# A post-norm layer kernel: the order of its last three chunks rearranged on VectorE, ScalarE and GpSimd

## What is computed

```python
# mixer: a gated linear recurrence over time, then RMS norm and a projection
r = sigmoid(x @ Wr.T); k = x @ Wk.T; v = x @ Wv.T
scale = exp(t * log(sigmoid(decay)))
state = cumsum(k * v / clip(scale, 1e-10)) * scale
x = layernorm(x + rmsnorm(r * state, ln_w) @ Wo.T)
# feed-forward with binarised weights (alpha = mean |w| of a row)
h = gelu(x @ (alpha1 * sign(w1)).T + b1)          # 1024 hidden features
out = layernorm(x + h @ (alpha2 * sign(w2)).T + b2)
```

## Time and profile before

| what | value |
|---|---|
| median of three runs | 821.32 us |
| the profiled execution | 821.34 us |
| its span, first to last instruction | 819.5 us |
| outside the span | 1.84 us |
| granted TensorE clock, mean | 0.998 of full |
| TensorE matmul busy | 797.3 us (97%) |
| VectorE busy | 773.9 us (94%) |
| ScalarE busy | 676.4 us (83%) |
| GpSimd busy | 296.8 us (36%) |

### The profile page before, as it was taken

The page is one execution under the profiler, slowest core; times in us unless marked ns, Lnnn a source line. Parts: engine busy times, 40 slices in busy tenths (PEclk is TensorE's granted clock), DMA queues, the critical chain, the costliest instruction groups (busy, mean ns, idle before and its releaser), DMA issues. The chain is left out here.

```text
span 819.5 us, 16560 instructions
## 1 busy us (share of the span) xinstructions
PE 797.3 (97%) x5173; PEld 505.5 (62%) x5173; DVE 773.9 (94%) x1473; ACT 676.4 (83%) x967; POOL 296.8 (36%) x567
## 2 busy tenths in 40 slices
PE   6989999999999999999999999999999999999995
PEld 4555666656666656666656666656666655666663
DVE  7998999999999999999999999999999999999997
ACT  7887888888888888888888888888888888887774
POOL 3343323343323344223344333344333344333345
PEclk9999999999999999999999999999999999999999
DMA  9514554444553544553534554434554444444313
GB/s 252 91 45 78 129 111 97 100 105 102 128 128 80 106 96 102 128 128 85 112 84 106 125 128 94 110 80 109 118 128 101 104 87 109 111 102 104 78 27 103
DMA packets 169846, 86.27 MB, mean 105 GB/s; under 512 B 130144, under 2 KB 165472, under 8 KB 169824
## 3 DMA queue, kind: packets, MB, share of 16 engines
q1 hardware_dynamic: 148560, 53.23, 30.1%
q0 software_dynamic: 4608, 16.78, 10.8%
q10 hardware_dynamic: 16656, 15.99, 5.7%
HBM read 20.45 MB, written 16.78 MB: 45 GB/s over the span
## 5 line engine op out<-in xcount | busy, mean ns | idle before, releaser
L481 PE MATMUL ps_o<-w2T,hid_hi 128*128 128x256 f16 x960 | 211.4, 273 | 2.2 <-DVE hid_lo L1027 2.1
L481 PE MATMUL ps_o<-w2T,hid_lo 128*128 128x256 f16 x960 | 211.4, 273 | 0.0
L363 PE MATMUL ps_r<-x_t,proj_hi 128*128 128x512 f16 x768 | 197.1, 379 | 1.9 <-DVE proj_lo L1125 1.4
L434 PE MATMUL ps_f<-x_t,w1T 128*128 128x512 f16 x768 | 181.8, 379 | 1.0 <-DVE x_t L1011 0.6
L688 ACT ACTIVATE hid<-ps_f,b1c,f_scale 128x512 f32<-128x512 f32 x192 | 145.5, 775 | 43.4 <-PE ps_f L434 38.3
L1027 DVE SCALAR_TENSOR_TENSOR hid_lo<-hid,hid_scale,hid_hi 128x1024 f16<-128x1024 f32 (+1 forms) x136 | 159.5, 1215 | 0.6 <-ACT hid_hi L728 0.6
L1352 POOL TENSOR_TENSOR y_sqs<-y_sq 128x512 f32<-128x512 f32 x32 | 46.7, 1460 | 308.4 <-ACT y_sq L656 308.4
L363 PEld LDWEIGHTS ps_r<-x_t,proj_hi 128*128 128x128 f16 x768 | 74.6, 98 | 92.2 <-issue 3.5
L728 ACT ACTIVATE hid_hi<-hid,hid_scale 128x2048 f16<-128x2048 f32 (+2 forms) x71 | 127.2, 1794 | 3.2
L434 PEld LDWEIGHTS ps_f<-x_t,w1T 128*128 128x128 f16 x768 | 74.9, 98 | 79.0 <-ACT hid L688 1.2
L363 PE MATMUL ps_r<-x_t,proj_lo 128*128 128x512 f16 x384 | 114.2, 379 | 0.0
(11 more groups left out here) (201 smaller groups left out, 1359.2 us busy)
## 6 DMA issues: line engine op xcount, KB each, us to landing
x_in<-in_L_attn_x_dram SPq DMA_DIRECT2D x32, 512.0 KB, 4.3
res<-b_row POOLq DMA_DIRECT2D x32, 512.0 KB, 4.6
out_dram<-res ACTq DMA_DIRECT2D x30, 512.0 KB, 3.1
w_in<-in_L_ffn_w_dram SPq DMA_DIRECT2D x2, 1024.0 KB, 9.9
x_t<-x_st SPq DMA_TRANSPOSE x59, 4.3
b_row<-in_L_ffn_b_dram SPq DMA_DIRECT2D x1, 512.0 KB, 13.1
out_dram<-res SPq DMA_DIRECT2D x1, 512.0 KB, 3.6
proj_in<-in_L_attn_Wk_dram SPq DMA_DIRECT2D x1, 256.0 KB, 4.9
```

What stands on the lines that cost most here:

```text
L363: last = nc.tensor.matmul(ps_r[:, m, :], w[:, m, dc, ec * P:(ec + 1) * P], xx[:, :, dc, :], start=(n == 0), stop=(n == 3 * DC - 1))
L434: last = nc.tensor.matmul(f1_bank[hc % NF], w1T[:, hc, dc, :], xx[:, :, dc, :], start=(dc == 0 and n == 0), stop=(dc == DC - 1 and n == 1))
L481: last = nc.tensor.matmul(o_tok[:, tt, :], hh[:, hc, tt * P:(tt + 1) * P], w2T[:, :, hc, :], start=(hc == 0 and n == 0), stop=(hc == HC - ...
```

## The change

- Step of chunk 29 (`left` 3). ScalarE does `yh` of chunk 31 after two `gelu` rather than three, and the high part of hidden tile 2 of chunk 30; GpSimd does tiles 3 and 4 instead of 2 and 3. VectorE does three `hl` ahead of `residual1` instead of two; `zadd` of chunk 29 moves from ahead of `yl` to behind the `hl`s; the two halves of `x1l_half` stand ahead of `zspread` and ahead of `zstats`. GpSimd runs the full `root_z` for chunk 29, and `x1b` waits for the DMA before it instead of for `zadd`.
- Step of chunk 30 (`left` 2). TensorE does four more matmuls ahead of the first half of `T1`. GpSimd does high parts 1 to 6 of chunk 31, ScalarE only 0 and 7. VectorE's `norm2` of chunk 29 is gone; ScalarE does it behind its last `hh`, ahead of `norm2` of chunk 30. VectorE's statistics of chunk 30 stand behind `hl` 0 and behind `hl` 3. `root_z` of chunk 30 waits for ScalarE's `norm2` of chunk 29 (`s_zout`).
- Step of chunk 31 (`left` 1). VectorE's `z_last` waits for `z_neg` of chunk 30 ahead of its first instruction, and then treats token tiles 0 and 1, tile 2, and tile 3 as three groups: multiply, add, statistics, aggregate, add epsilon into `last_ve`. GpSimd no longer adds. It takes a root for each group into `last_rstd`, and `last_shift` for the first group, which ScalarE uses. The new tensors take the place of `z_rstd` and `z_shift` for this chunk.

The diff (declarations and most unchanged lines are left out):

```diff
@@ -249,7 +252,7 @@
-        POOL_TILES = [[2, 3], [1, 2, 4, 5, 6]]
+        POOL_TILES = [[3, 4], [1, 2, 3, 4, 5, 6]]
         ACT_TILES = [[h for h in range(HC) if h not in tiles] for tiles in POOL_TILES]
@@ -499,8 +502,9 @@
                     products(range(TT), hc)
+                products((0, 1), HC - 3)
                 T1(c + 1, (j + 1) % CPB, False, (0, 1))
-                products(range(TT), HC - 3)
+                products((2, 3), HC - 3)
                 T1(c + 1, (j + 1) % CPB, False, (2, 3))
@@ -716,11 +720,11 @@
-            def norm2(c, j, shifts=1, tts=range(TT)):
-                act.wait_ge(s_zshift, c + shifts)
+            def norm2(c, j, tts=range(TT), shift=z_shift, rstd=z_rstd):
+                act.wait_ge(s_zshift, c + 1)
                 for tt in tts:
                     nc.scalar.activation(res[j][:, tt, :], res[j][:, tt, :], ACT.Identity,
-                                         bias=z_shift[:, tt:tt + 1], scale=z_rstd[:, tt:tt + 1]).then_inc(s_zout, 1)
+                                         bias=shift[:, tt:tt + 1], scale=rstd[:, tt:tt + 1]).then_inc(s_zout, 1)
@@ -861,11 +865,10 @@
                     if left > 2:
-                        gelu(i + 1, range(0, 3))
+                        gelu(i + 1, range(0, 2))
                         yh(i + 2)
-                        gelu(i + 1, range(3, 4))
                     for part in tile_groups(left - 1):
-                        if part.start > 3 or left == 2:
+                        if part.start > 1 or left == 2:
                             gelu(i + 1, range(part.start, part.stop))
@@ -873,9 +876,10 @@
                 if left == 2:
-                    norm2(i, j, shifts=0)
+                    norm2(i - 1, j - 1)
+                    norm2(i, j)
                 if left == 1:
-                    norm2(i, j, shifts=0, tts=range(TT // 2))
+                    norm2(i, j, range(TT // 2), last_shift, last_rstd)
                     store_first(i, j)
@@ -1042,49 +1046,32 @@
-                dve.wait_ge(s_f2, 2 * c + 2)
-                nc.vector.tensor_tensor(z_t[:, 0:2, :], ps_o[:, 0:2, 0:D], alpha2_row[:, :, :],
-                                        ALU.mult).then_inc(s_zmul, 1)
                 dve.wait_ge(s_x1b, 16 * c + 16)
-                dve.wait_ge(s_zneg, c - 1)
-                def added(n, tt):
-                    dve.wait_ge(s_f2, 2 * c + tt + 1)
-                    nc.vector.tensor_tensor(z_t[:, tt, :], z_bank[tt], alpha2_row[:, 0, :],
+                dve.wait_ge(s_zneg, c)
+                groups = [(slice(0, 2), ps_o[:, 0:2, 0:D]), (slice(2, 3), ps_r[:, 0:1, 0:D]),
+                          (slice(3, 4), ps_r[:, 1:2, 0:D])]
+                for n, (tts, src) in enumerate(groups):
+                    dve.wait_ge(s_f2, 2 * c + tts.stop)
+                    nc.vector.tensor_tensor(z_t[:, tts, :], src, alpha2_row[:, 0:tts.stop - tts.start, :],
                                             ALU.mult).then_inc(s_zmul, 1)
...
+                    dve.wait_ge(s_zmul, 2 * c + n + 1)
+                    nc.vector.tensor_tensor(res[j][:, tts, :], z_t[:, tts, :], res[j][:, tts, :],
                                             ALU.add).then_inc(s_zadd, 1)
...
-                def moments(tts, made):
...
+                    for tt in range(tts.start, tts.stop):
+                        nc.vector.bn_stats(z_st[:, tt, :], res[j][:, tt, :]).then_inc(s_zst, 1)
+                    dve.wait_ge(s_zst, TT * c + tts.stop)
                     stand_alone(dve)
...
+                    for tt in range(tts.start, tts.stop):
                         nc.vector.bn_aggr(z_mv[:, tt, :], z_st[:, tt, :]).then_inc(s_zmv, 1)
-                    dve.wait_ge(s_zmv, TT * c + made)
...
-                added(0, 2)
-                for tt in range(TT // 2):
-                    dve.wait_ge(s_zfirst, tt + 1)
...
-                moments((0, 1, 2), 3)
-                added(1, 3)
-                moments((3,), TT)
+                    dve.wait_ge(s_zmv, TT * c + tts.stop)
+                    nc.vector.tensor_scalar_add(last_ve[:, tts], z_mv[:, tts, 1], EPS_LN).then_inc(s_last_ve, 1)
...
                 for n, tt in enumerate(range(TT // 2, TT)):
-                    dve.wait_ge(s_zrstd, c + n + 1)
+                    dve.wait_ge(s_zrstd, c + n + 2)
                     nc.vector.tensor_scalar(res[j][:, tt, :], res[j][:, tt, :], z_mv[:, tt, 0:1],
-                                            z_rstd[:, tt:tt + 1], ALU.subtract, ALU.mult).then_inc(s_zlast, 1)
...
-            def norm2(c, j):
-                dve.wait_ge(s_zrstd, c + 1)
-                for tt in range(TT):
-                    nc.vector.tensor_scalar(res[j][:, tt, :], res[j][:, tt, :], z_mv[:, tt, 0:1],
...
+                                            last_rstd[:, tt:tt + 1], ALU.subtract, ALU.mult).then_inc(s_zlast, 1)
@@ -1094,7 +1081,7 @@
                 if apart:
-                    dve.wait_ge(s_zout, TT * c + TT)
+                    dve.wait_ge(s_zneg, c)
                 dve.wait_ge(s_zst, TT * c + TT)
@@ -1253,7 +1240,7 @@
                 if left == 2:
-                    for part in parts[:2]:
+                    for part in parts[:3]:
                         hl(i, part, 0)
@@ -1270,12 +1257,13 @@
                     nc.vector.tensor_scalar_mul(u_neg[:, :], u_mv[:, :, 0], -1.0).then_inc(s_uneg, 1)
-                    for part in parts[2:]:
+                    for part in parts[3:]:
                         hl(i, part, 0)
+                    zadd(i - 1, (j - 1) % CPB)
+                    x1l_half(i + 1, 0)
                     zspread(i - 1, (j - 1) % CPB, range(2))
-                    x1l_half(i + 1, 0)
+                    x1l_half(i + 1, 1)
                     zstats(i - 1, (j - 1) % CPB, range(2, TT))
-                    x1l_half(i + 1, 1)
@@ -1288,7 +1276,7 @@
                     block_sums(i + 2)
-                if left > 1:
+                if left > 3 or left == 2:
                     zadd(i, j)
@@ -1303,12 +1291,11 @@
                     hl(i + 1, parts[0], 1)
-                    norm2(i - 1, j - 1)
-                    hl(i + 1, parts[1], 1)
                     zspread(i, j, range(2))
-                    hl(i + 1, parts[2], 1)
+                    for part in parts[1:4]:
+                        hl(i + 1, part, 1)
                     zstats(i, j, range(2, TT), apart=True)
-                    for part in parts[3:]:
+                    for part in parts[4:]:
                         hl(i + 1, part, 1)
@@ -1329,10 +1316,13 @@
-            def x1b(c, j):
+            def x1b(c, j, last=False):
...
                 pool.wait_ge(s_x1l, c + 1)
-                pool.wait_ge(s_zadd, c + 1)
+                if last:
+                    pool.wait_ge(s_x1b, 16 * c)
+                else:
+                    pool.wait_ge(s_zadd, c + 1)
                 pool.sem_inc(s_issued, 1)
@@ -1392,40 +1382,35 @@
-            def z_root(c):
+            def root_z(c):
                 pool.wait_ge(s_zmv, TT * c + TT)
...
                 nc.gpsimd.tensor_tensor(z_rstd[:, :], z_ve[:, :], neg_half[:, :], ALU.pow).then_inc(s_zrstd, 1)
...
-            def root_z(c, shifts=1):
-                z_root(c)
                 nc.gpsimd.tensor_scalar(z_neg[:, :], z_mv[:, :, 0], -1.0, 1.0, ALU.mult, ALU.mult).then_inc(s_zneg, 1)
                 pool.wait_ge(s_zrstd, c + 1)
-                pool.wait_ge(s_zneg, c + shifts)
+                pool.wait_ge(s_zneg, c + 1)
                 nc.gpsimd.tensor_tensor(z_shift[:, :], z_neg[:, :], z_rstd[:, :], ALU.mult).then_inc(s_zshift, 1)
...
                 first = slice(0, 2)
-                pool.wait_ge(s_x1b, 16 * c + 16)
-                pool.wait_ge(s_zmul, 2 * c + 1)
-                for tt in range(TT // 2):
-                    nc.gpsimd.tensor_tensor(res[j][:, tt, :], z_t[:, tt, :], res[j][:, tt, :],
-                                            ALU.add).then_inc(s_zfirst, 1)
-                pool.wait_ge(s_zout, TT * c + TT)
-                pool.wait_ge(s_zve_tile, 1)
-                nc.gpsimd.tensor_tensor(z_rstd[:, 0:3], z_ve[:, 0:3], neg_half[:, 0:3], ALU.pow).then_inc(s_zrstd, 1)
+                pool.wait_ge(s_last_ve, 1)
+                nc.gpsimd.tensor_tensor(last_rstd[:, first], last_ve[:, first], neg_half[:, first],
+                                        ALU.pow).then_inc(s_zrstd, 1)
+                pool.wait_ge(s_zshift, c)
                 nc.gpsimd.tensor_scalar(z_neg[:, first], z_mv[:, first, 0], -1.0, 1.0, ALU.mult,
...
                 pool.wait_ge(s_zrstd, c + 1)
-                pool.wait_ge(s_zneg, c)
-                nc.gpsimd.tensor_tensor(z_shift[:, first], z_neg[:, first], z_rstd[:, first],
+                pool.wait_ge(s_zneg, c + 1)
+                nc.gpsimd.tensor_tensor(last_shift[:, :], z_neg[:, first], last_rstd[:, first],
                                         ALU.mult).then_inc(s_zshift, 1)
-                pool.wait_ge(s_zve_tile, 2)
```

(42 more changed lines are left out.)

3 lines of the change are left out of this document (1 added, 2 removed).

## The result

| | before | after |
|---|---|---|
| median | 821.23 us (821.07 to 821.36, 8 runs) | 823.30 us (823.11 to 825.54, 8 runs) |
| profiled execution, its span | 821.34, 819.5 us | 825.54, 823.7 us |
| granted TensorE clock in it | 0.998 | 0.994 |

The ratio is 1.0035, with a 95% interval of 1.0023 to 1.0046: 2.1 us slower, where no change was forecast. The changed kernel's eight times form two groups, five at 823.1 to 823.3 us and three at 825.4 to 825.5 us. The profile is of the second group.

The account below looks back on a forecast made before the run. With TensorE 97% and VectorE 94% busy, only the end was taken to matter, chiefly VectorE's chain: 821.34 + 1.0 (z_last later) + 0.25 (z_last longer) - 1.3 (last store) = 821.3 us, range 819.5 to 822.6.

Parts of the forecast that it names:

- Front: Chunks 29 to 31: the new order starts F1 of chunk 31 at 795.6, 0.64 us earlier.
- Without collisions: Middle, if GpSimd and VectorE did not block each other: z_last at 808.1, the z_neg wait taking 0.9 of 1.6 us.
- With GpSimd: Middle, with hl and GpSimd's high parts excluding each other: z_last at 809.6 to 809.95, 0.8 to 1.15 us later.
- From there high parts and `hl`s take turns: Chunk 31, from GpSimd's high part 1 at 800.9 to 801.6: alternation with VectorE at 1.1 to 1.29 us a pair.
- the forecast's lower end: Chunk 31, if GpSimd always gets in first: VectorE's last hl ends at 808.95; otherwise 809.3.
- TensorE's last products: End of chunk 31: products after the last hl add 0.65 us before z_last starts.
- The rule of the lock: Middle: VectorE instructions with two SBUF inputs and GpSimd instructions reading SBUF take one lock; the loser blocks.
- TensorE's clock: F2 of chunk 31: thinly spaced products drop the clock to 1.2 GHz, giving 823.4 us; rival, chance 0.08.
- The new wait: Ahead of z_last: z_neg of chunk 30 comes at 809.0 to 809.75, just hidden.
- Tail: z_last in three groups: 6.3 us instead of 6.06, 0.25 longer.
- Stores: Last store lands in 1.7 us instead of 3.0, no longer sharing DMA engines: 1.3 us gained, at least 0.7.

Follow-up runs that it names:

- front-and-tail run: The changed kernel with the middle put back as in the kernel before, keeping only the new front and tail: 820.98 us against 821.11 before.
- late-start run: The changed kernel with GpSimd's first high part of chunk 31 also waiting for the gelu of tile 4, so starting after the DMA issue: 821.58 us.
- TensorE kept busy: The changed kernel with 20 and 10 idle transposes, results unread, added between TensorE's products of chunk 31: 823.13 us.
- three on GpSimd and the wait moved: The changed kernel with GpSimd doing only high parts 1, 3, 5 of chunk 31 and z_last's z_neg wait moved to its first aggregation: 820.97 us.
- The run without the first store: The kernel before, with the 256 KB store of token tiles 0 and 1 of the last chunk left out: 820.39 us against 821.01.

## Why the prediction was wrong, step by step

- **Front.** Right: `y_hi` at 780.26, `norm1` at 790.93, F1 at 795.61, against 780.32, 790.95 and 795.6. That it is worth little by itself, the front-and-tail run shows.
- **Without collisions.** Not reached, but its order was right: ScalarE's `norm2` of chunk 29 ended at 806.21 (806.3 said), high part 1 at 801.53 (801.6). But that high part took 1.01 us from 800.52, inside the DMA issue, where 0.7 from 800.9 was said: the lead stood behind a right number.
- **With GpSimd: here it failed.** The step is "From there high parts and `hl`s take turns". I had it that whoever gets in first, the other gets in next, and took 1.1 to 1.29 us a pair as both ends. One more order was possible, in which GpSimd gets in every time: six high parts 0.65 us apart, then `hl`. That costs 1.5 us more on `z_last`, 811.3 instead of the 809.6 to 809.95. The late-start run removes GpSimd's lead, at the price of a start 0.53 us later, and gives 809.75 and 821.58 us, where I had forecast 809.8 and 821.3. So the step fits the kernel without the lead. Its last `hl` ends at 808.95, the forecast's lower end. TensorE's last products add 0.80 us in it, not 0.65; the store is below.
- **The rule of the lock.** Right as far as it went: `hl` and high part exclude each other wherever they meet in the kept traces. The Trainium skill's page SBUF — State Buffer, "Who interferes with whom", says the loser blocks, and also that issue order decides who blocks. By the starts in the trace that second rule does not hold in the changed kernel: the second `hl` started at 801.56, and the high parts that started at 801.86 and later went ahead of it. Starts are all that the trace shows; how the lock is granted stays open. I took alternation from two high parts in the earlier trace rows, too short a stretch to show it.
- **TensorE's clock.** The rival with a chance of 0.08, priced at 823.4 us on top of a `z_last` near 809.8, came in three runs of eight on top of the shut-out. Its price of 2.1 us (823.4 - 821.3) measured 2.2, and that was luck: it was to be 0.45 us on `z_last` and 1.7 on tile 3, and came as 2.26 on `z_last` and nothing behind it (6.33 us in the profile after, 6.34 with TensorE kept busy). Ahead of the fall TensorE idled 2.29 us in one piece, where the forecast had gaps below a microsecond. That alone doesn't explain the fall: in the late-start kernel, whose pace was the forecast one, the longest piece is 1.20 us and three of ten runs were longer at a lower mean clock; with three on GpSimd and the wait moved it is 1.20 us too, and no run was. What decides between runs of one kernel stays open.
- **The new wait.** "Just hidden", `z_neg` at 809.0 to 809.75, was right in sign: it ended at 810.54 with `z_last` at 811.3 or later. With the shut-out gone it binds in two runs (waits of 1.3 and 1.55 us), at 0.73 us where it was priced.
- **Tail.** Right: 6.33 us against 6.3.
- **Stores.** The direction was right and the term too large: 0.9 of 1.3 us, as it landed in 2.1 and not 1.7. In the other traces with the new tail it landed in 1.8 to 2.0, and once in 2.4. The prediction's estimate of 2.3 us for 128 KB rests on a section of the Trainium skill's page DMA: Bandwidth & Descriptors that describes DMAs issued by GpSimd; this store is issued by SP. The run without the first store bears the sharing out, with 1.02 us between the profiled executions and 0.62 between the medians.

Open stays why GpSimd gets its lead. It is there in the changed kernel, where the `z_shift` of chunk 29, itself slowed by the first `hl`, stands right ahead of the DMA issue; not in the kernel before or in the late-start run. And that the lead is the cause, and not only its mark, rests on one run that removed it and on one that lacked it. It takes a queue as well: with two or three high parts on GpSimd the first has the lead too (800.52 with three), and VectorE gets in.

## What to carry to other kernels

Where two engines exclude each other, ask not only what one pair costs but how long the other's queue of ready work is: a helper that can run six instructions in a row may hold the main engine for all six. Space its work by what it waits for, or give it every second tile; and put a wait right ahead of the instruction that needs it, since cover that hides it may go. A stretch in which TensorE starves can cost twice, once for the work that comes late and once for the clock at which it then runs.

## What was unexpected of the hardware

- One `hl` stood for 3.79 us behind five more high parts of GpSimd, each of which had started 0.29 to 0.34 us before its predecessor ended; with starts 0.01 to 0.02 us ahead the same instructions took turns (1.17 to 1.18 us for the longest `hl`).
- A GpSimd instruction is recorded as started at 800.52 while the DMA issue ahead of it in the same list ends at 800.77.
- The same kernel was granted half the TensorE clock for 6.5 us in the profiled run; two more of its eight runs were as long, with the same mean clock of 0.994, and five were 2.2 us shorter at 0.996 to 0.998.
